# Stage six of an eight-stage transformer kernel: token rows gathered by an inverse list instead of sent to slots, and the shared expert squared and kept by ScalarE

## The chip, the cores and the metric

The kernel runs on one core of one Trainium2 chip as a single program. The metric is device microseconds (us) of one execution; lower is better. The kernel before was timed three times: 1947.86, 1949.66 and 1950.64 us, median 1949.66.

## The reference, cut to what matters

The whole program is four layers of attention and feed-forward blocks over a residual `x` of 4 batches x 512 tokens x 256 features in f32. The change is in the feed-forward block of the third layer, the program's sixth stage: a mixture of experts with a shared expert, on layer-normed tokens.

```python
logits = x @ w_router.T                       # 2048 tokens, 8 experts
probs = softmax(logits)
expert_weight, expert_idx = top_k(probs, 2)
expert_weight = expert_weight / sum(expert_weight, axis=-1)
# tokens sorted by expert; each expert e, on its own tokens:
inter = square(relu(x_e @ w1[e].T))           # 256 -> 256
outb  = inter @ w2[e].T                       # 256 -> 256
moe_out = zeros.at[token].add(outb * weight)  # two contributions a token
sh = square(relu(h @ ws1.T))                  # 256 -> 512, every token
shared_out = sh @ ws2.T                       # 512 -> 256
return shared_out + moe_out                   # added to the residual
```

The eighth stage is another mixture of experts (gated, 704 hidden features) with the same routing of 2 out of 8.

## The kernel before, in words

Each engine runs its own instruction list in order, and semaphores tie the lists together. The stages follow one another with a barrier of all engines between them. `core.x`, the residual, stays in SBUF; PSUM is one tensor `ps` of 8 banks of 512 f32 columns.

Stage six is `relu_experts_stage` (L2348). The 2 x 2048 choices are laid out in blocks of N = 256 slots, each block of one expert; K = 23 blocks always run, so that any distribution fits.

- **Router** (L1941, unchanged): layer norm of 16 token tiles into `kept_rows`, transposes into `xT`, logits, softmax, the two best. VectorE then computes in `Slots.vector_places` (L2265 to L2312) each choice's slot, each block's expert (`expert_no`, semaphore `experts_known`) and a copy of each token row for each of its two choices (`out_rows`: 256 features, the destination number, the weight; 32 instructions at L2312).
- **Sending**: GpSimd (`pool_send`, L2166) scatters these with 32 indirect DMAs of 128 rows into `xs_rows` in device memory. Unused slots must hold valid spare numbers, so stage five fills all of `xs_rows` from the constant `blank_rows` (L1635) beforehand. SyncE waits for all 32 and then loads each block of 256 rows (`xs`, L2109).
- **The shared expert** is cut into 8 units (half of the hidden features x a batch). `shared_first(u)` (L2414) is 4 f32 matmuls of 512 columns into banks 0 and 1; ScalarE takes relu (L2481), VectorE squares (L2526); `shared_second(u)` (L2425) is 8 f32 matmuls into banks 4 to 7; VectorE adds each tile to the residual (L2536). Six units (`FRONT`) run before the block loop and two behind it. TensorE's order is first(1), second(0), first(2), second(1), and so on.
- **The block loop**, software pipelined, per block k on TensorE: `up(k+1)` (L2445), the transposes of block k+2 (L2209), `down(k)` (L2456). ScalarE: relu (`gate`, L2490) of k+1, then the weighted result of k (L2499). VectorE: the square of k+1 (`product`, L2548), then two tiny copies of numbers and weights (L2319, L2321) and the tokens of k+2 to SBUF (L2551). GpSimd: a cast of the numbers (L2174) and two indirect DMAs that write the results of k to `y_rows` (L2179), so 46 in all. SyncE: per block one load of w1, one of w2, one of xs. The loops are hardware loops with register indices.
- **Collecting**: after the last write SyncE loads `y_rows` back in 8 loads of 512 KB (L2153); VectorE adds them to the residual (L2343), in order behind the additions of the shared units.

Stage eight uses another class, `Places` (L2563), which sends no rows. SyncE writes the normed rows once, in order, to `xn_rows` (L2620). VectorE marks for each choice its tile and its lane as f16 zeros and ones (`tile_is`, `lane_is`); TensorE's `tensor_inverse` (L2660) turns them into inverse lists with 32 matmuls for the numbers (L2667) and 32 for the weights (L2673), the latter from three f16 parts that GpSimd makes (`pool_weights`, L2632 to L2643). Results are `x_no` (which token row each slot reads), `y_no` (where its result goes) and `weight_of`. GpSimd then gathers each block's rows with two indirect DMAs (`gather`, L2858), four blocks ahead, and writes the block's results with two more (`give_back`, L2865), all in one unrolled list.

Of the kernel before, what the change touches and what calls it, by code (L numbers as in the profile page):

```python
# [20 lines left out]
P = 128  # L21
B = 4
# [1528 lines left out]
def autocorrelation_stage(core):  # L1551
# [19 lines left out]
    with Stage(core, "l2x") as st:  # L1571
# [30 lines left out]
        out_full, rows_added, cleared = st.sem("out_full"), st.sem("rows_added"), st.sem("rows_cleared")  # L1602
# [6 lines left out]
        def _(sp):  # L1609
# [25 lines left out]
            sp.dma_start(dram["xs_rows"], dram["blank_rows"]).then_inc(cleared, 16)  # L1635
# [8 lines left out]
            sp.wait_ge(cleared, 16)  # L1644
# [396 lines left out]
class Slots:  # L2041

    E = 8
    T = B * TT
    N = 2 * P
    K = (2 * T * P + E * (N - 1)) // N
    W = D + 2
    LOOPED = (K - 2) // 2

    def __init__(self, st, router, scaled):  # L2060

        T, E, K, W, N = self.T, self.E, self.K, self.W, self.N
        U32 = mybir.dt.uint32
        self.nc, self.core, self.router, self.scaled, self.dram = st.nc, st.core, router, scaled, st.core.dram
        self.earlier, self.ones = st.sb("earlier", [P, P]), st.sb("ones", [P, P])
        self.numbers = st.sb("numbers", [P, T, 2])
        self.starts = st.sb("starts", [P, E])
        self.block_no = st.sb("block_no", [P, K])
        self.y_in = st.sb("y_in", [P, 2, T, D])
        self.slot, self.is_second = (st.sb(n, [P, T, E]) for n in ("slot", "is_second"))  # L2070
        self.sums = st.sb("sums", [P, 2, T, E])
        self.filled = st.sb("filled", [P, E, E])
        self.blocks, self.ends, self.counts = st.sb("blocks", [P, E]), st.sb("ends", [P, 2, E]), st.sb("counts", [P, E])
        self.ended = st.sb("ended", [P, K, E])
        self.expert, self.expert_no = st.sb("expert", [P, K]), st.sb("expert_no", [P, K], I32)
        self.slots, self.slot_no = st.sb("slots", [P, T, 2]), st.sb("slot_no", [P, T, 2], U32)
        self.slot_sum = st.sb("slot_sum", [P, T])
        self.weight = st.sb("weight", [P, T, 2])
        self.out_rows = st.sb("out_rows", [P, T, 2, W])
        self.xs = st.sb("xs", [P, 2, 2, W])  # L2080
        if not scaled:
            self.xT = st.sb("xT_block", [P, 2, DC, N])
        self.y = st.sb("y", [P, 2, 2, D])
        self.numbers_of, self.weight_of = st.sb("numbers_of", [P, K, 2]), st.sb("weight_of", [P, K, 2])
        self.row_no = st.sb("row_no", [P, 2, 2], U32)
        self.const_in, self.ones_ready = st.sem("const_in"), st.sem("ones_ready")
        self.placed, self.ranks_full, self.experts_known = st.sem("placed"), st.sem("ranks_full"), st.sem("experts_known")
        self.rows_ready, self.scattered = st.sem("rows_ready"), st.sem("scattered")
        self.xs_in = [st.sem(f"xs_in{i}") for i in range(2)]
        self.turned, self.xT_ready = st.sem("turned"), st.sem("xT_ready")  # L2090
        self.y_ready, self.row_no_ready = st.sem("y_ready"), st.sem("row_no_ready")
        self.y_out = [st.sem(f"y_out{i}") for i in range(2)]
        self.y_back = [st.sem(f"y_back{b}") for b in range(B)]
        self.added = st.sem("added")

    def sync_constants(self, sp):
        dram = self.dram
        for dst, name in ((self.earlier, "earlier"), (self.numbers, "choice_numbers")):  # L2100
            sp.dma_start(dst[:], dram[name]).then_inc(self.const_in, 16)
        sp.dma_start(self.starts[:], dram["block_starts"].to_broadcast([P, self.E])).then_inc(self.const_in, 16)
        sp.dma_start(self.block_no[:], dram["block_numbers"].to_broadcast([P, self.K])).then_inc(self.const_in, 16)

    def sync_expert(self, sp, k):
        return sp.value_load(self.expert_no[0:1, bass.ds(k, 1)], min_val=0, max_val=self.E - 1)

    def sync_tokens(self, sp, r, i):
        sp.dma_start(self.xs[:, i, :, :],  # L2109
                     self.dram["xs_rows"][bass.ds((r * 2 + i) * self.N, self.N), :].rearrange("(j p) d -> p j d", p=P)  # L2110
                     ).then_inc(self.xs_in[i], 16)

    def sync_blocks(self, sp, first, second):

        K = self.K

        def second_of(r, i):
            second(self.sync_expert(sp, r * 2 + i), r, i)

        def step(r, i, left=3):
            first(self.sync_expert(sp, r * 2 + i), r, i)
            if left > 1:
                sp.wait_ge(self.xT_ready, r * 2 + i)
                self.sync_tokens(sp, r + i, 1 - i)
            second_of(r - 1 + i, 1 - i)

        sp.wait_ge(self.experts_known, 1)
        first(self.sync_expert(sp, 0), 0, 0, wait=False)
        second_of(0, 0)
        first(self.sync_expert(sp, 1), 0, 1, wait=False)
        sp.wait_ge(self.scattered, 2 * self.T * 16)
        for i in range(2):
            self.sync_tokens(sp, 0, i)
        sp.wait_ge(self.xT_ready, 1)
        self.sync_tokens(sp, 1, 0)
        with sp.Fori(1, (K - 1) // 2) as r:  # L2140
            for i in range(2):
                step(r, i)
        for k in range((K - 1) // 2 * 2, K):
            step(k // 2, k % 2, left=K - k)
        second_of((K - 1) // 2, (K - 1) % 2)

    def sync_collect(self, sp):
        for i in range(2):
            sp.wait_ge(self.y_out[i], 32 * ((self.K + 1 - i) // 2))
        for b in range(B):  # L2150
            for c in range(2):
                at = (c * B + b) * S
                sp.dma_start(self.y_in[:, c, b * TT:(b + 1) * TT, :],  # L2153
                             self.dram["y_rows"][at:at + S, :].rearrange("(j p) d -> p j d", p=P)).then_inc(self.y_back[b], 16)

    def pool_ones(self, pool):
        self.nc.gpsimd.memset(self.ones[:], 1.0).then_inc(self.ones_ready, 1)
        pool.wait_ge(self.ones_ready, 1)  # L2160

    def pool_send(self, pool):
        for t in range(self.T):
            pool.wait_ge(self.rows_ready, t + 1)
            for c in range(2):
                self.nc.gpsimd.indirect_dma_start(  # L2166
                    self.dram["xs_rows"], bass.IndirectOffsetOnAxis(ap=self.slot_no[:, t, c:c + 1], axis=0),
                    self.out_rows[:, t, c, :], None).then_inc(self.scattered, 16)

    def pool_return(self, pool, r, i):  # L2170
        k = r * 2 + i

        pool.wait_ge(self.y_ready, k + 1 + 2)
        self.nc.gpsimd.tensor_copy(self.row_no[:, i, :], self.numbers_of[:, bass.ds(k, 1), :].rearrange("p o j -> p (o j)")  # L2174
                                   ).then_inc(self.row_no_ready, 1)
        pool.wait_ge(self.row_no_ready, k + 1)
        pool.nop(nofuse=True)
        for c in range(2):
            self.nc.gpsimd.indirect_dma_start(  # L2179
                self.dram["y_rows"], bass.IndirectOffsetOnAxis(ap=self.row_no[:, i, c:c + 1], axis=0),  # L2180
                self.y[:, i, c, :], None).then_inc(self.y_out[i], 16)

    def pool_return_all(self, pool):
        with pool.Fori(0, self.K // 2) as r:
            for i in range(2):
                self.pool_return(pool, r, i)
        for k in range(self.K // 2 * 2, self.K):
            self.pool_return(pool, k // 2, k % 2)

    def tensor_ranks(self, pe):

        nc, ps, TE = self.nc, self.core.ps, self.T * self.E
        pe.wait_ge(self.const_in, 64)
        pe.wait_ge(self.ones_ready, 1)
        pe.wait_ge(self.placed, 1)
        nc.tensor.matmul(ps[:, 3, 0:TE], self.earlier[:], self.router.chosen[:].rearrange("p t e -> p (t e)"),
                         start=True, stop=False)
        nc.tensor.matmul(ps[:, 3, 0:TE], self.ones[:], self.sums[:, 1].rearrange("p t e -> p (t e)"), start=False, stop=True)  # L2200
        nc.tensor.matmul(ps[:, 4, 0:self.E], self.ones[:], self.sums[:, 0, self.T - 1, :], start=True, stop=True
                         ).then_inc(self.ranks_full, 1)
# [143 lines left out]


def relu_experts_stage(core):  # L2348

# [1359 lines left out]
```

## Time and profile before

| what | value |
|---|---|
| median of the three timed runs | 1949.66 us |
| the profiled execution, its own time | 1950.97 us |
| its span | 1949.2 us |
| TensorE busy / VectorE / ScalarE / GpSimd | 1621.0 / 1039.4 / 851.6 / 527.2 us |
| mean granted TensorE clock | 0.898 |
| stage six, first to last instruction | 688.9 to 910.3 us |

Times in the profile are microseconds from the span's start. PE is TensorE's matmuls, PEld its weight loads, DVE VectorE, ACT ScalarE, POOL GpSimd, SP SyncE; L2445 is line 2445 of the kernel. The chain of waits that ended last is followed back only as far as 1577 us, into stage eight, so stage six has to be read from its own timeline. In a windows row the columns are: stretch, its length, busy microseconds (and instructions) of PE, PEld, DVE, ACT and POOL, then granted TensorE clock (1.00 is 2.4 GHz, 0.50 is 1.2 GHz), DMA share and GB/s.

### The profile page before, as it was taken

The numbers are of one execution on the slowest core, as the hardware profiler recorded it, in microseconds if no ns is written. First come the engines' busy times: TensorE is split into PE (matmuls) and PEld (weight loads), VectorE is DVE, ScalarE is ACT, GpSimd is POOL, SyncE is SP. The second block draws the span as 40 slices with busy tenths as digits, with TensorE's granted clock in tenths as the row PEclk, the third lists the DMA queues.
The fourth block names the chain that finished last, engine by engine and source line by source line (L and its number), as shares of the span: only waits on it lengthen the run. The fifth ranks groups of instructions, "written<-read, shape, count | busy, mean of one in ns | idle before, by whom it ended". The sixth has DMA issues, their size and how long they took to land. (4 is left out here: it accounts for less than half of the span.)

```text
span 1949.2 us, 30637 instructions
## 1 busy us (share of the span) xinstructions
PE 1621.0 (83%) x10659; PEld 1079.1 (55%) x10662; DVE 1039.4 (53%) x2717; ACT 851.6 (44%) x1771; POOL 527.2 (27%) x564
## 2 busy tenths in 40 slices
PE   6999549782569968894899999999999973999994
PEld 2233238561246555673456656746756673888883
DVE  6543464557764155336586377378456536444443
ACT  2767203033512111231577277367557611555551
POOL 2000100001251007342337108206504505233321
PEclk8999866895889969997899999999999975999997
DMA  3000200201070103686213104203302213677785
GB/s 124 1 1 1 68 11 1 86 1 45 1 251 23 38 24 104 197 250 207 80 40 131 48 1 139 80 1 105 125 1 70 81 47 103 219 239 239 230 232 169
DMA packets 90977, 185.91 MB, mean 95 GB/s; under 512 B 10560, under 2 KB 56512, under 8 KB 90504
## 3 DMA queue, kind: packets, MB, share of 16 engines
q1 hardware_dynamic: 73320, 125.85, 19.9%
q0 software_dynamic: 17536, 58.51, 8.9%
q8 instruction: 68, 1.11, 0.2%
q14 instruction: 53, 0.43, 0.1%
HBM read 146.01 MB, written 44.40 MB: 98 GB/s over the span
## 5 line engine op out<-in xcount | busy, mean ns | idle before, releaser
L3452 ACT ACTIVATE l3x_prob<-l3x_biased,l3x_neg_max 128x512 f32<-128x512 f32 x256 | 183.8, 721 | 39.3 <-DVE l3x_neg_max L3548 35.7
L3548 DVE CUSTOM_DVE_ANT_0 l3x_biased<-ps,l3x_mask 128x512 f32<-128x512 f32 x256 | 173.4, 681 | 13.6 <-PE ps L3326 6.8
L2907 PE MATMUL ps<-l3f_x_hi,l3f_w 128*128 128x256 f16 x1012 | 171.5, 274 | 3.8 <-DVE l3f_x_lo L3034 2.4
L402 ACT ACTIVATE l0x_prob<-ps 128x1024 f32<-128x1024 f32 x128 | 122.6, 1027 | 80.1 <-PE ps L347 80.0
L3336 PE MATMUL ps<-ident,l3x_prob 128*128 128x128 f32 x1024 | 142.0, 282 | 1.1 <-ACT l3x_prob L3452 1.0
L2907 PE MATMUL ps<-l3f_x_lo,l3f_w 128*128 128x256 f16 x506 | 138.8, 274 | 0.0
L3461 ACT ACTIVATE l3x_probT<-ps 128x512 f32<-128x512 f32 x192 | 112.1, 586 | 42.2 <-PE ps L3336 42.2
L3352 PE MATMUL ps<-l3x_probT,l3x_v 128*64 128x256 f32 x1024 | 124.6, 385 | 5.0 <-ACT l3x_probT L3461 5.0
L3336 PEld LDWEIGHTS ps<-ident,l3x_prob 128*128 128x128 f32 x1024 | 111.3, 142 | 27.8 <-issue 21.2
L3023 DVE TENSOR_TENSOR l3f_h<-l3f_silu,ps 128x256 f32<-128x256 f32 x115 | 48.4, 421 | 141.0 <-ACT l3f_silu L2972 140.9
L2907 PEld LDWEIGHTS ps<-l3f_x_hi,l3f_w 128*128 128x128 f16 x1012 | 99.6, 98 | 18.8 <-issue 4.4
L2921 PE MATMUL ps<-l3f_w,l3f_h_hi 128*128 128x256 f16 x552 | 96.2, 274 | 0.0
L2865 POOL DMA_INDIRECT y_rows<-l3f_y,l3f_y_no x46 | 45.4, 988 | 181.9 <-ACT l3f_y L2981 174.9
L3352 PEld LDWEIGHTS ps<-l3x_probT,l3x_v 128*64 128x64 f32 x1024 | 67.8, 136 | 47.3 <-issue 11.8
L3559 DVE COPY l3x_probT<-ps 128x512 f32<-128x512 f32 x64 | 44.2, 690 | 88.7 <-PE ps L3336 87.8
L3323 PE MATMUL ps<-l3x_k_hi,l3x_q 128*128 128x512 f16 x256 | 78.0, 386 | 13.2 <-DVE l3x_neg_max L3548 13.1
L2972 ACT ACTIVATE l3f_silu<-ps 128x256 f32<-128x256 f32 x138 | 52.7, 382 | 82.2 <-PE ps L2907 80.6
L3249 PE MATMUL ps<-l3x_x_hi,l3x_w 128*128 128x512 f16 x256 | 82.6, 384 | 0.0
L3092 POOL TENSOR_TENSOR l3x_raw_parts<-l3x_raw,l3x_raw_parts 128x1088 f16<-128x1088 f32 x32 | 72.2, 2256 | 2.7
L367 PE MATMUL ps<-l0x_prob,l0x_v 128*32 128x512 f32 x512 | 68.0, 604 | 3.0 <-DVE l0x_oT L456 2.5
L3426 ACT ACTIVATE l3x_q<-ps 64x512 f16<-64x512 f32 x64 | 37.8, 591 | 61.0 <-PE ps L3249 60.6
L3220 POOL CAST l3x_o_hi<-l3x_o 128x256 f16<-128x256 f32 x64 | 28.1, 439 | 131.4 <-DVE l3x_o L3530 131.4
(611 smaller groups left out, 3669.8 us busy)
## 6 DMA issues: line engine op xcount, KB each, us to landing
l3f_w<-l3f_parts SPq DMA_DIRECT2D x23, 1408.0 KB, 6.8
l3f_w<-l3f_parts SPq DMA_DIRECT2D x23, 768.0 KB, 6.3
l3x_raw<-in_l3f_weights POOLq DMA_DIRECT2D x32, 544.0 KB, 4.0
l3f_parts<-l3x_raw_parts POOLq DMA_DIRECT2D x32, 544.0 KB, 3.2
l2f_w<-in_l2f_w SPq DMA_DIRECT2D x46, 256.0 KB, 3.1
xs_rows<-in_blank_rows SPq DMA_DIRECT2D x1, 5934.0 KB, 25.3
l2f_xs<-xs_rows SPq DMA_DIRECT2D x23, 258.0 KB, 3.3
l2f_y_in<-y_rows SPq DMA_DIRECT2D x8, 512.0 KB, 7.0
```

Source lines behind the costliest of these rows:

```text
L367: last = nc.tensor.matmul(ps[r:r + 32, AV_BANK, :], values[:, b % 2, j, 4 * g + head, :, :], probs[:, head, :], start=(j == 0 and at == 0) ...
L402: nc.scalar.activation(prob[:, n % KEPT, 2 * h:2 * h + 2, :], ps[:, bank:bank + 2, :], ACT.Sigmoid, scale=0.25).then_inc(prob_ready, 1)
L2907: last = nc.tensor.matmul(ps[:, f % RING, g * N:(g + 1) * N], w13[:, i, part, c * 2 * F + at:c * 2 * F + at + P], x[:, i, c, :], start=(n ...
L2921: last = nc.tensor.matmul(ps[:, 4 + i, j * D:(j + 1) * D], hT[0:m, i, f, j * P:(j + 1) * P], w2[0:m, i, part, f * D:(f + 1) * D], start=(n ...
L3092: G.tensor_tensor(lo, raw, hi, ALU.subtract).then_inc(self.lo_made, 1)
L3249: last = nc.tensor.matmul(out, a, b, start=(begin and n == 0), stop=(end and n == len(passes) - 1))
L3323: nc.tensor.matmul(ps[:, (u + i) % 3, :], q2[:, 2 * hp + i, tile], k_hi[:], start=True, stop=False)
L3336: last = nc.tensor.transpose(ps[:, turned_bank(unit), s * P:(s + 1) * P], prob[:, unit % 4, s * P:(s + 1) * P], core.ident[:])
L3352: last = nc.tensor.matmul(ps[rows, av_bank(group), 0:HALF].rearrange("p (j q) -> p j q", j=2), v[:, s, :], probT[:, group % 2, :, i, s * P ...
L3452: nc.scalar.activation(prob[:, unit % 4, :], biased[:, unit % 4, :], ACT.Exp, scale=-1.0, bias=neg_max[:, u // 4, u % 4:u % 4 + 1], accum_ ...
L3461: nc.scalar.activation(prob_slot(made), ps[:, turned_bank(made), :], ACT.Copy).then_inc(copied[0], 1)
L3548: V.tensor_tensor_reduce(out=biased[:, unit % 4, :], in0=ps[:, u % 3, :], in1=mask[:, u % 8 // 2, :], scale=-1.0, scalar=3.0e38, op0=ALU.a ...
```

## The change: what it does

Class `Slots` goes, and with it `xs_rows`, its blank fill in stage five, the 32 sends, the 32 row copies, the 23 loads of `xs` and the per-block copies and casts of numbers. Stage six now uses `Places`, whose `tensor_inverse` is split into two calls, with the bank of the numbers as a parameter. The order of the shared units is now by batch (both halves of a batch one after the other, summed in PSUM); ScalarE squares as well, and copies the sum of a batch out of PSUM (`keep`) once per batch; VectorE adds that copy once per batch. All loops but SyncE's are written out. The last units and the collection stay where they were.

```diff
@@ stage five
-            sp.dma_start(dram["xs_rows"], dram["blank_rows"]).then_inc(cleared, 16)
-            sp.wait_ge(cleared, 16)
@@ class Places
-    def tensor_inverse(self, pe):
+    def tensor_numbers(self, pe):
...
+    def tensor_weights(self, pe):
@@ relu_experts_stage, GpSimd
+            def gather(k):
+                if k >= AHEAD:                       # AHEAD = 4
+                    pool.wait_ge(turned, k - AHEAD + 1)
+                for j in range(2):
+                    nc.gpsimd.indirect_dma_start(
+                        gathered[:, k % AHEAD, j, :], None, dram["xn_rows"],
+                        bass.IndirectOffsetOnAxis(ap=places.x_no[:, 2 * k + j:2 * k + j + 1], axis=0)).then_inc(rows_in[k % AHEAD], 16)
+            def give_back(k):
+                pool.wait_ge(y_ready, k + 1)
+                for j in range(2):
+                    nc.gpsimd.indirect_dma_start(
+                        dram["y_rows"], bass.IndirectOffsetOnAxis(ap=places.y_no[:, 2 * k + j:2 * k + j + 1], axis=0),
+                        y[:, k % 2, j, :], None).then_inc(y_out[k % 2], 16)
+            places.pool_ones(pool)
+            router.pool(pool)
+            places.pool_weights(pool)
+            pool.wait_ge(places.rows_out, 16 * B)
+            pool.wait_ge(places.numbers_known, 1)
+            for k in range(AHEAD):
+                gather(k)
+            for k in range(K):
+                if k + AHEAD < K:
+                    gather(k + AHEAD)
+                give_back(k)
@@ TensorE
+            for u in range(FRONT):
+                if u + 1 < FRONT:
+                    shared_first(u + 1)
+                shared_second(u)
+                if u == 3:
+                    places.tensor_numbers(pe)
+                if u == 4:
+                    places.tensor_weights(pe)
+            pe.wait_ge(shared_kept, FRONT // 2)
...
+            turn(0)
+            up(0)
+            turn(1)
+            for k in range(K):
+                if k + 1 < K:
+                    up(k + 1)
+                if k + 2 < K:
+                    turn(k + 2)
+                down(k)
+            pe.wait_ge(relu_ready, K)
+            shared_first(FRONT)
+            pe.wait_ge(y_ready, K)
+            for u in range(FRONT, UNITS):
+                if u + 1 < UNITS:
+                    shared_first(u + 1)
+                shared_second(u)
@@ ScalarE
+            def hidden(u):
+                for f in range(FT):
+                    n = u * FT + f
+                    act.wait_ge(shared_up, n + 1)
+                    A.activation(relu[:, u % 2, f, :], ps[:, n % 2, :], ACT.Relu).then_inc(shared_relu, 1)
+                ...
+                for f in range(FT):
+                    A.activation(hT[:, u % 2, f, :], relu[:, u % 2, f, :], ACT.Square).then_inc(shared_hidden, 1)
+            def keep(b):
+                act.wait_ge(shared_down, 2 * b + 2)
+                bank = 4 + b % 2 * 2
+                A.activation(shared_rows[:, b, :, :], ps[:, bank:bank + 2, :]..., ACT.Copy).then_inc(shared_kept, 1)
+            def result(k):
+                act.wait_ge(down_full, k + 1)
+                if k >= 2:
+                    act.wait_ge(y_out[k % 2], k // 2 * 32)
+                ...
@@ VectorE, behind places.vector_places
+            for b in range(FRONT // 2):
+                add_shared(b)                        # waits for shared_kept, b + 1
+            tokens(0)
+            product(0)
+            tokens(1)
+            for k in range(K - 1):
+                product(k + 1)
+                if k + 2 < K:
+                    tokens(k + 2)
+            for b in range(FRONT // 2, B):
+                add_shared(b)
+            dve.wait_ge(shared_added, B)
+            for b in range(B):
+                dve.wait_ge(y_back[b], 32)
+                ...                                  # two additions of y_in, as before
@@ SyncE: per block w1 once up(k-2) is done, then w2 once down(k-2) is done
```

## Rows read from the trace of the kernel before

**Rows 1.** The windows view of stage six: microseconds busy per engine, clock, DMA.

```profile
748.40:779.50 31.10, 31.10 (x113) 21.04 (x111) 13.60 (x28) 4.78 (x8) 23.49 (x23) 1.00 0.29 103
...
791.00:885.10 94.10, 92.71 (x445) 75.09 (x446) 31.35 (x85) 31.58 (x66) 44.43 (x64) 1.00 0.77 233
885.10:910.30 25.20, 13.78 (x49) 8.78 (x47) 15.85 (x20) 3.23 (x6) 4.39 (x5) 0.82 0.57 187
```

**Rows 2.** The timeline (start, us, engine, line, what) of the shared expert's front.

```profile
730.89 5.16 PE L2414 MATMUL ps<-l2f_xT,l2f_ws 128*128 128x512 f32 x8 [2.97 <-DVE l2f_expert_no L2292]
...
742.17 6.34 PE L2425 MATMUL ps<-l2f_ws,l2f_hT_shared 128*128 128x256 f32 x16 [6.12 <-DVE l2f_hT_shared L2526]
...
755.23 3.60 PE L2414 MATMUL ps<-l2f_xT,l2f_ws 128*128 128x512 f32 x8
...
762.12 3.60 PE L2414 MATMUL ps<-l2f_xT,l2f_ws 128*128 128x512 f32 x8
```

**Rows 3.** The timeline where the block loop begins: first transposes, first return.

```profile
783.36 1.09 PE L2209 MATMUL ps<-ident,l2f_xs 128*128 128x128 f32 x4 [3.85 <-DMA l2f_xs<-xs_rows]
...
797.29 0.96 POOL L2179 DMA_INDIRECT y_rows<-l2f_y,l2f_row_no  x1 [0.79 <-POOL l2f_row_no L2174]
```

**Rows 4.** The timeline of one block of stage six in the steady loop.

```profile
803.71 2.00 PE L2445 MATMUL ps<-l2f_xT_block,l2f_w 128*128 128x256 f32 x8
...
805.74 0.60 ACT L2490 ACTIVATE l2f_relu<-ps 128x512 f32<-128x512 f32 x1 [1.00 <-PE ps L2445]
...
806.37 0.69 DVE L2548 TENSOR_TENSOR l2f_hT<-l2f_relu 128x512 f32<-128x512 f32 x1 [2.72 <-ACT l2f_relu L2490]
...
807.12 0.68 DVE L2551 COPY l2f_xT_block<-ps 128x512 f32<-128x512 f32 x1
...
807.86 1.99 PE L2445 MATMUL ps<-l2f_xT_block,l2f_w 128*128 128x256 f32 x8
...
808.09 0.84 ACT L2499 ACTIVATE l2f_y<-ps,l2f_weight_of 128x256 f32<-128x256 f32 x2 [1.75 <-PE ps L2456]
```

**Rows 5.** Stage eight's timeline: first and last of four consecutive indirect DMAs.

```profile
1684.79 1.00 POOL L2865 DMA_INDIRECT y_rows<-l3f_y,l3f_y_no  x1 [6.92 <-ACT l3f_y L2981]
...
1688.67 0.96 POOL L2858 DMA_INDIRECT l3f_gathered<-xn_rows,l3f_x_no  x1 [0.30 <-issue]
```

**Rows 6.** The eighth stage's gather line (L2858): time from issue to landing.

```profile
DMA to landing us min/median/max: 2.7/3.6/4.6
```

**Rows 7.** The timeline where an indirect DMA starts inside a two-input VectorE product.

```profile
759.50 0.69 DVE L2526 TENSOR_TENSOR l2f_hT_shared<-l2f_relu_shared 128x512 f32<-128x512 f32 x1 [1.02 <-ACT l2f_relu_shared L2481]
759.61 1.41 POOL L2166 DMA_INDIRECT xs_rows<-l2f_out_rows,l2f_slot_no  x1 [0.30 <-issue]
```

**Rows 8.** Stage eight's timeline: experts' numbers, then the list-making matmuls.

```profile
1618.55 0.18 DVE L2713 TENSOR_SCALAR l3f_expert_no<-l3f_expert 128x23 int32<-128x23 f32 x1
...
1637.24 1.41 PE L2667 MATMUL ps<-l3f_marked_values,l3f_lane_is 128*128 128x92 f16 x16 [3.18 <-DVE l3f_lane_is L2748]
...
1639.76 3.86 PE L2673 MATMUL ps<-l3f_marked_values,l3f_lane_is 128*128 128x138 f16 x32 [1.11 <-POOL l3f_marked_values L2643]
```

**Rows 9.** The windows view of a stretch of the list-making matmuls.

```profile
1639.70:1643.70 4.00, 3.86 (x32) 3.58 (x32) 0.00 (x0) 0.00 (x0) 2.74 (x4) 0.50 0.17 49
```

**Rows 10.** The page: a two-bank ScalarE read, and the expert weight loads.

```profile
L402 ACT ACTIVATE l0x_prob<-ps 128x1024 f32<-128x1024 f32 x128 | 122.6, 1027 | 80.1 <-PE ps L347 80.0
...
l2f_w<-in_l2f_w SPq DMA_DIRECT2D x46, 256.0 KB, 3.1
```

**Rows 11.** The windows view of stage five while the blank fill runs.

```profile
575.00:580.00 5.00, 5.00 (x18) 3.11 (x17) 2.89 (x10) 0.87 (x3) 4.23 (x4) 1.00 0.95 342
```

**Rows 12.** The timeline of stage six's end.

```profile
884.94 7.03 PE L2414 MATMUL ps<-l2f_xT,l2f_ws 128*128 128x512 f32 x16
...
892.70 7.39 SPq L2153 DMA_DIRECT2D l2f_y_in<-y_rows  x8
...
907.77 2.48 DVE L2343 TENSOR_TENSOR x_sb<-x_sb,l2f_y_in 128x1024 f32<-128x1024 f32 x2 [0.44 <-DMA l2f_y_in<-y_rows]
```

More of the change, by code:

```diff
@@ L1601, in autocorrelation_stage @@
         agg_full, agg_by_act, agg_by_vector = st.sem("agg_full"), st.sem("agg_by_act"), st.sem("agg_by_vector")
-        out_full, rows_added, cleared = st.sem("out_full"), st.sem("rows_added"), st.sem("rows_cleared")
+        out_full, rows_added = st.sem("out_full"), st.sem("rows_added")
         block = st.block()
@@ L2575, with __init__ @@
     PARTS = 5
-    def __init__(self, st, router):
+    def __init__(self, st, router, numbers_bank=5):
         T, E, K = self.T, self.E, self.K
+        self.numbers_bank = numbers_bank
         U32 = mybir.dt.uint32
@@ L2666, in tensor_inverse @@
                 pe.wait_ge(self.lanes_marked, n // T + 1)
-            last = nc.tensor.matmul(ps[:, 5, 0:4 * K], self.lane_is[:, n, :],
+            last = nc.tensor.matmul(ps[:, self.numbers_bank, 0:4 * K], self.lane_is[:, n, :],
                                     self.marked[:, n, 0:2, :].rearrange("p v k -> p (v k)"),
@@ L2670, in tensor_inverse @@
         last.then_inc(self.numbers_full, 1)
+    def tensor_weights(self, pe):
+        nc, ps, K, T = self.nc, self.core.ps, self.K, self.T
         pe.wait_ge(self.weights_marked, 3)
@@ L2752, in vector_places @@
         dve.wait_ge(self.numbers_full, 1)
-        token, second = ps[:, 5, 0:2 * K], ps[:, 5, 2 * K:4 * K]
+        bank = self.numbers_bank
+        token, second = ps[:, bank, 0:2 * K], ps[:, bank, 2 * K:4 * K]
         V.tensor_scalar(self.x_no[:], token, -1.0, 0.0, ALU.add, ALU.max)
@@ L2886, in _ @@
             places.tensor_ranks(pe)
-            places.tensor_inverse(pe)
+            places.tensor_numbers(pe)
+            places.tensor_weights(pe)
             def turn(r, i):
```

611 lines of the change are left out of this document (184 added, 427 removed).

## The prediction

> **What bounds the kernel now.** The page's chain of waits is followed back only into stage eight, so I read stage six by the windows view first and then by its timeline. The windows [rows 1] show three stretches with different limits. While the shared expert's front runs (748.4 to 779.5) TensorE is busy all the time at full clock. In the block loop (791.0 to 885.1) it is busy 92.7 of 94.1 us, while GpSimd is busy 44.4: TensorE and the VectorE link into it set the pace. Behind it (885.1 to 910.3) TensorE works 13.8 of 25.2 us, and the write-back and its re-load end last. Two stalls lie ahead of the loop: 6.12 us before second(0), which waited for VectorE's square behind the 32 row copies [rows 2], and 3.85 us before the first transposes, which waited for the sends and the load of xs [rows 3].
>
> One block's circle reads as follows [rows 4]: up starts 803.71, relu 805.74 to 806.34, square 806.37 to 807.06, two tiny copies, tokens 807.12 to 807.80, next up 807.86. One round is 4.15 us.
>
> **The front, until the first return.** experts_known doesn't move: the instructions ahead of it are the same but for constants. From there on:
> - first(1): 730.89 + 5.16 (half of it at the low clock) = 736.05 [rows 2].
> - second(0) follows at once, since ScalarE has squared unit 0 long before. One unit (first and second) takes 762.12 - 755.23 = 6.89 us, 3.60 of it first, so second takes 3.29 [rows 2]: 739.3. Before, it began at 742.17 and took 6.34, cold; here TensorE has not rested, and the level holds (the windows give 1.00 for unbroken work [rows 1]).
> - Three units: 20.7, so 760.0.
> - The 32 matmuls for the numbers: 2 x 1.41 = 2.8 us in stage eight, those for the weights 3.86 [rows 8]. That was at clock 0.50 [rows 9], the 1.2 GHz level; at 2.4 GHz no row shows them. Between half of it and all of it, I take half (the stretch around them runs at 1.00): 1.4 and 1.9. Their inputs: in stage eight the second half waited for VectorE until 1637.24, 18.5 us after the experts' numbers (1618.73), and the weights for GpSimd until 1639.76, 21.0 us after [rows 8]; here 29 and 37 us pass, so neither waits: 761.4.
> - first(5) and second(4) 6.9, weights 1.9, second(5) 3.3: 773.5.
> - keep(2): a two-bank ScalarE read, nearest row 1.03 us [rows 10] and 0.2 for the hand-over: 774.8, and TensorE may start turn(0). VectorE adds batch 2 (one of the two halves of the 2.48 us in [rows 12], 1.24), copies tokens (0.68, [rows 4]): up(0) at 776.9.
> - One round to up(1), one to the end of down(0): 785.2. Result 0.84 [rows 4] and 0.2: 786.2. GpSimd's first return starts at 786.4 instead of 797.29 [rows 3]: 10.9 us gained. Uncertain by +3.3 us (lists at the low clock) and some 0.5 the other way.
>
> Squares on ScalarE appear in no row; nearest is the relu of 0.60 [rows 4]. Two of them behind a relu are 1.8 us, and first(u+1) covers 3.6. Even at double price they are hidden. Without that cover each of the 8 units would pay up to 2 us.
>
> **The block loop.** Here the change adds what costs most. GpSimd had two indirect DMAs and a cast per block; now it has four indirect DMAs. In stage eight four in a row start at 1684.79 and 1688.67, the last 0.96 long with 0.30 to the next: 1689.93 - 1684.79 = 5.14 us [rows 5]. In stage six one takes 0.96, so four would be 5.04 [rows 3]. Both are above TensorE's 4.15, so GpSimd becomes the bound. I take 5.14, the row with the same mix. The wait for y_ready(k) has gather(k+4) behind it, which TensorE's turn(k+4) needs only four blocks later, and y_out(k-2) lands well within two rounds, so GpSimd isn't starved in mid-loop. The two tiny copies that VectorE loses (0.14 a round) and the xs load that SyncE loses bring nothing, as they lie beside GpSimd. SyncE now asks for w1 only behind w2, a wait of down(k-2) instead of up(k-1): landing 3.1 us [rows 10] within a round of 5.14 leaves 2 us for its register loads.
>
> From 786.4 GpSimd does 18 returns and 18 gathers (blocks 5 to 22): 18 x 5.14 = 92.5, so 878.9. The last gather, issued 1.26 earlier, lands 3.6 later [rows 6]: 881.2. TensorE's part of a round is up 2.0 and turn with down 2.15 (together 4.15, [rows 4]); a down alone is half of a second, 1.7 [rows 2]. turn(22) and down(20) 2.15, up(22) 2.0, down(21) 1.7, down(22) 1.7: 888.8. y_ready(21) comes at 887.1 + 1.0 = 888.1; four more DMAs behind it, 5.1: 893.3. Before, the last ended 891.2, 1.5 ahead of SyncE's re-load at 892.70 [rows 12]. So the 10.9 us are used up and 2.1 more.
>
> **The end.** The re-load starts at 894.8; its last part was awaited until 15.1 us after its start (907.77 - 892.70 [rows 12]), so 909.9. But shared units 6 and 7 come behind down(22) on TensorE: before it began them at 884.94 [rows 12], now at 888.8. 13.8 us for both [rows 1]: 902.6. Then keep(3) 1.2 (903.8) and VectorE's addition 1.24 (905.0), and only behind it the eight additions, 4 x 2.48 = 9.9 [rows 12]: 914.9 instead of 910.25. Those additions were spaced by landings before; now VectorE sets the end.
>
> Stage five loses the blank fill, but its TensorE was busy 5.00 of 5.00 us in the middle of it [rows 11]: nothing to gain. Bounds 0 to -1.
>
> **Sum.** Against the profiled execution (1950.97, span 1949.2): -10.9 front, +13.0 loop, +2.6 end = +4.7, 1955.7. It lay 1.3 above the median of the runs, so 1949.66 + 4.7 = 1954.4. A change within 0.2% (3.9 us) is about what a measurement can't tell from none.
>
> **Rivals.**
> A. *VectorE holds GpSimd up as well, slower still.* An indirect DMA that starts 0.11 us into a VectorE product with both inputs in SBUF took 1.41 instead of 0.96 [rows 7]. In the loop the square is such a product, 0.69 us a round. Starts come every 1.28, so with free phase about every second round is hit for 0.3: 18 x 0.14 = +2.5; if the phase locks on it, 18 x 0.45 = +8.1. For: the square follows the landing of gathers, so the phase is fixed by GpSimd itself. Against: the return in [rows 3] and the gather in [rows 5] have 0.96, and the sum's 5.14 may hold some of it already. Time 1957 to 1962.5.
> The Trainium skill (GPSIMD Engine Reference, section Key points) says the same: contention of the shared SBUF interfaces arises with VectorE instructions that have two SBUF inputs; by that rule alone the time would be the upper one, 1962.5, if every round is hit. [Rows 7] agree in one instance.
> B. *The other side: GpSimd doesn't bound.* It would have to overlap issue with the next DMA, or hold the lead of its four early gathers. Then the round is 4.0 (4.15 less what the tiny copies took): y_ready(22) = 786.2 + 22 x 4.0 = 874.2, down(22) 873.2, units 887.0, end 899.3, thus -10.9 and 1939. It decides from a round below 4.88 (18 x 0.26 = 4.7 cancels my sum). Against: in no row do two indirect DMAs start less than 1.25 apart.
> C. *The front gives less:* lists at the low clock and cold first blocks, 3.3 to 4 us: 1958.
> D. *Equal:* DMAs at 1.25 (round 5.0, -2.5) and up to 1 us less at the end, if keep and additions come cheaper: 1951.
>
> **Chances.** Forecast 0.47 (own range 1952 to 1958), A 0.20, B 0.10, C 0.10, D 0.13. Faster than 1945.8: B and a little of other cases, 0.12. Within 0.2%: most of D and the lower part of the forecast, up to 1953.6, 0.27. Slower: 0.61. The range to hold 8 in 10: 1947 to 1964.
>
> **What would show it.** Right: in the loop GpSimd nearly always busy, with 1.25 to 1.3 between starts and rounds of 5.0 to 5.3; TensorE's clock and busy share down, with waits for gathered rows or for ScalarE's result; no 6.12 us stall ahead of second(0); first return near 786; VectorE's eight additions in one piece of 10 us behind keep(3). Wrong: rounds below 4.8 us; list matmuls that wait for VectorE or GpSimd; ScalarE's squares on TensorE's waits; a w1 load awaited; stage five shorter by more than 1 us.

## The result and the profile after

The changed kernel takes 1962.75 us (median; 1962.5 to 1963.14) against 1949.66 before: a ratio of 1.0069, 95% interval 1.0046 to 1.0092. Run again with more rounds it came to 1.0055 (1.0042 to 1.0069). So it is slower by 11 to 13 us, where +4.7 was predicted. Direction and cause of the forecast hold; its size is less than half of what happened. The 1962.75 lies in the range given for 8 in 10 (1947 to 1964) and outside the forecast's own (1952 to 1958).

A stage's length is read from its first layer-norm instruction to that of the next stage. The view by tile gives them, for the kernel before (first pair) and the changed one (second pair); the number ahead of "to" is the first start in us.

```profile
L117 DVE BATCH_NORM_STATS2 l2f_bn<-x_sb x16: 407/409/428, 689.0 to 699.3; 128x6 f32<-128x256 f32 x16
L117 DVE BATCH_NORM_STATS2 l3x_bn<-x_sb x16: 395/408/427, 911.5 to 1309.7; 128x6 f32<-128x256 f32 x16
```

```profile
L117 DVE BATCH_NORM_STATS2 l2f_bn<-x_sb x16: 408/410/428, 687.7 to 698.1; 128x6 f32<-128x256 f32 x16
L117 DVE BATCH_NORM_STATS2 l3x_bn<-x_sb x16: 395/409/428, 922.8 to 1321.4; 128x6 f32<-128x256 f32 x16
```

Stage six went from 222.5 to 235.1 us, 12.6 more; in its second run 232.1, with the blank fill put back (below) 233.1. The mean of the three is 233.4: +10.9. What follows the stage has the same length, 1037.7 and 1037.6 us. What precedes it varies by 4.6 us from run to run whatever the kernel (685.2 to 689.8 over all runs here), so times below are compared from the stage's own start.

The windows view of the changed kernel answers to [rows 1]: start and end, length, busy us (instructions) of PE, PEld, DVE, ACT, POOL, then clock, DMA share, GB/s. The windows are the shared front, the block loop and the end.

```profile
729.80:775.20 45.40, 44.21 (x200) 29.97 (x200) 21.82 (x34) 14.23 (x23) 25.40 (x16) 0.94 0.17 47
790.00:880.00 90.00, 74.61 (x352) 59.81 (x353) 22.28 (x35) 25.36 (x53) 68.54 (x69) 0.98 0.69 200
881.50:921.50 40.00, 25.32 (x95) 18.24 (x93) 13.08 (x12) 10.04 (x19) 9.78 (x11) 0.85 0.55 167
```

TensorE, busy 92.7 of 94.1 us in the old loop, is now busy 74.6 of 90. GpSimd has 69 instructions there; 68.54 busy and 0.30 between each two (69 x 0.30 = 20.7) make 89.2 of the 90 us, so it is the engine that hardly rests.

The timeline of the front, to be read against [rows 2, 3]: second(0) follows first(1) without the stall of 6.12, the matmuls for the numbers start at 760.23, and the first return at 786.53. But first(1) takes 6.40 instead of 5.16.

```profile
729.88 6.40 PE L2368 MATMUL ps<-l2f_xT,l2f_ws 128*128 128x512 f32 x8 [2.98 <-DVE l2f_expert_no L2194]
736.12 3.62 PE L2379 MATMUL ps<-l2f_ws,l2f_hT_shared 128*128 128x256 f32 x16
...
760.23 1.48 PE L2144 MATMUL ps<-l2f_marked_values,l2f_lane_is 128*128 128x92 f16 x32
763.39 1.19 POOL L2332 DMA_INDIRECT l2f_gathered<-xn_rows,l2f_x_no  x1 [12.57 <-DVE l2f_y_no L2241]
774.13 1.02 ACT L2463 ACTIVATE l2f_shared_rows<-ps 128x1024 f32<-128x1024 f32 x1 [7.25 <-PE ps L2379]
775.21 0.66 PE L2401 MATMUL ps<-ident,l2f_gathered 128*128 128x128 f32 x4 [1.11 <-ACT l2f_shared_rows L2463]
...
786.53 1.01 POOL L2339 DMA_INDIRECT y_rows<-l2f_y,l2f_y_no  x1 [8.04 <-ACT l2f_y L2484]
```

The windows view of first(1), before and after, shows why: after the same 3 us of rest the mean granted clock is 0.56 instead of 0.71, so more of it ran at the 1.2 GHz level.

```profile
730.89:736.05 5.16, 5.15 (x8) 2.06 (x8) 4.88 (x23) 0.60 (x1) 1.20 (x1) 0.71 0.43 118
```

```profile
729.88:736.10 6.22, 6.22 (x8) 2.66 (x9) 5.74 (x19) 0.60 (x1) 2.89 (x5) 0.56 0.51 148
```

The timeline inside the loop: two returns and two gathers a block, and the next block's first return 5.2 us later. One return of 1.49 us starts 0.07 into VectorE's product with two SBUF inputs, as in [rows 7].

```profile
814.63 0.69 DVE L2525 TENSOR_TENSOR l2f_hT<-l2f_relu 128x512 f32<-128x512 f32 x1 [3.07 <-ACT l2f_relu L2476]
814.70 1.49 POOL L2339 DMA_INDIRECT y_rows<-l2f_y,l2f_y_no  x1 [0.30 <-issue]
...
829.75 1.00 POOL L2339 DMA_INDIRECT y_rows<-l2f_y,l2f_y_no  x1 [0.30 <-issue]
831.05 0.99 POOL L2339 DMA_INDIRECT y_rows<-l2f_y,l2f_y_no  x1 [0.30 <-issue]
832.35 0.99 POOL L2332 DMA_INDIRECT l2f_gathered<-xn_rows,l2f_x_no  x1 [0.30 <-issue]
833.64 1.03 POOL L2332 DMA_INDIRECT l2f_gathered<-xn_rows,l2f_x_no  x1 [0.30 <-issue]
834.98 1.00 POOL L2339 DMA_INDIRECT y_rows<-l2f_y,l2f_y_no  x1 [0.31 <-issue]
```

TensorE's waits from 775 to 905 (us in total, times, longest). The loads of w1 come first. The prediction had dismissed them, and had named an awaited w1 load among the signs that it was wrong:

```profile
PE ps L2412 <- DMA l2f_w<-in_l2f_w: 12.5, 12, 3.0
PE ps L2401 <- DMA l2f_gathered<-xn_rows,l2f_x_no: 5.5, 6, 1.7
```

The timeline of the end, against [rows 12]: w1 of block 21 is asked for at 878.97, 1.22 us behind a load of w2; up(21) waits for it until 884.25 and then runs partly at the low level, the last return is over at 899.5 instead of 891.2, and the eight additions run in one piece behind keep(3) and the shared addition.

```profile
877.75 0.38 SPq L2305 DMA_DIRECT2D l2f_w<-in_l2f_w  x1
...
878.97 0.38 SPq L2299 DMA_DIRECT2D l2f_w<-in_l2f_w  x1
...
881.81 1.00 POOL L2339 DMA_INDIRECT y_rows<-l2f_y,l2f_y_no  x1 [0.31 <-issue]
...
884.25 2.57 PE L2412 MATMUL ps<-l2f_xT_block,l2f_w 128*128 128x256 f32 x8 [2.27 <-DMA l2f_w<-in_l2f_w]
...
898.53 0.97 POOL L2339 DMA_INDIRECT y_rows<-l2f_y,l2f_y_no  x1 [0.30 <-issue]
...
901.01 0.38 SPq L2323 DMA_DIRECT2D l2f_kept_rows<-y_rows  x1
...
909.12 1.02 ACT L2463 ACTIVATE l2f_shared_rows<-ps 128x1024 f32<-128x1024 f32 x1 [5.27 <-PE ps L2379]
910.18 1.23 DVE L2513 TENSOR_TENSOR x_sb<-x_sb,l2f_shared_rows 128x1024 f32<-128x1024 f32 x1 [16.93 <-ACT l2f_shared_rows L2463]
911.44 1.22 DVE L2544 TENSOR_TENSOR x_sb<-x_sb,l2f_kept_rows 128x1024 f32<-128x1024 f32 x1
...
920.26 1.23 DVE L2544 TENSOR_TENSOR x_sb<-x_sb,l2f_y_second 128x1024 f32<-128x1024 f32 x1
```

### The profile page after: what moved, and what is told of

Read it like the earlier page. It is cut to its first block and busy times, and to the rows that moved or that the text cites. A ratio compares the mean times of both kernels' runs of the same rounds, so it can differ in the third digit from the quotient of the medians.

```text
span 1960.4 us, 30184 instructions
## 1 busy us (share of the span) xinstructions
PE 1625.3 (83%) x10723; PEld 1084.1 (55%) x10726; DVE 1026.8 (52%) x2612; ACT 865.3 (44%) x1791; POOL 554.1 (28%) x563
## 5 line engine op out<-in xcount | busy, mean ns | idle before, releaser
L137 POOL TENSOR_TENSOR l3x_rstd<-l3x_var,neg_half 128x4 f32<-128x4 f32 x4 | 4.1, 1036 | 214.9 <-DVE l3x_var L124 214.9
```

## The experiments

Each starts from the changed kernel. Ratios are to the kernel before, timed beside it on the same chip; "length" is that of stage six, from each run's own trace (before 222.5, changed 233.4 as the mean of three). A length is one execution, and the three of the changed stage lie 3.0 us apart, so small differences are read from the ratios.

| run | ratio, 95% interval | length |
|---|---|---|
| changed, again | 1.0055 [1.0042, 1.0069] | 232.1 |
| w1 asked first | 1.0059 [1.0045, 1.0073] | 231.9 |
| one-input product | 1.0055 [1.0039, 1.0070] | 233.2 |
| blank fill back | 1.0048 [1.0033, 1.0064] | 233.1 |
| VectorE squares | 1.0153 [1.0137, 1.0168] | 250.8 |
| 8 gather buffers | 1.0038 [1.0024, 1.0051] | 229.5 |
| half the gathers | 1.0009 [1.0000, 1.0018] | 222.9 |
| half the gathers, w1 first | 0.9940 [0.9925, 0.9956] | 210.9 |
| deep | 0.9984 [0.9975, 0.9993] | 218.2 |
| deep, 4 units ahead | 0.9949 [0.9936, 0.9963] | 211.3 |
| the same, w1 late | 0.9996 [0.9987, 1.0005] | 221.7 |
| the same, w1 first, 7 y buffers | 0.9916 [0.9903, 0.9930] | 205.8 |

**The changed kernel again**

> The changed kernel itself once more, to have its ratio to the kernel before from more rounds: the runs that undo one part of it (the fill 1.0048, the w1 order 1.0059) lie inside the interval of its first measurement, 1.0046 to 1.0092. Expected 1.0055 to 1.0070, stretches of 1.1 to 1.5 us on five to eight of the indirect DMAs of the loop, and 18 rounds in 94.5 to 96 us. If it comes out at 1.0048 or less, the fill and the w1 order at the loop's end are worth nothing that can be measured.

1.0055; 18 rounds of GpSimd in 94.3 us, from 784.23 to 878.52, just under the 94.5 to 96 expected. The first measurement's profile was on the long side, by 3 us of stage length. The ratio of this run lies within the intervals of the next three and theirs within its own, so none of the three moved the time measurably.

**w1 asked for before w2**

```diff
+            first(1, 0)
             with sp.Fori(1, K // 2) as r:
                 for i in range(2):
-                    first(r, i)
+                    first(r + i, 1 - i)
                     second(r, i)
             for k in range(K // 2 * 2, K):
-                first(k // 2, k % 2)
                 second(k // 2, k % 2)
```

> SyncE asks for w1 of block k+1 before w2 of block k, as the kernel before did; all else is the changed kernel. Theory G (GpSimd's four indirect DMAs, 5.17 us a round, set the loop, and the w1 order costs only at its end): TensorE's waits for w1 go from 12.5 us to under 2 us, the gaps turn into waits for rows or for GpSimd, the returns still come every 5.17 us, and only the end of the loop gains, 2 to 5 us: 1958 to 1961. Rival W (the late w1 sets the round): the returns come every 4.2 to 4.6 us and the time falls by 10 us or more, to 1952 or less. Rival V (VectorE's product holds GpSimd up): no change but the end's.

TensorE's waits for w1 are gone. The same idle time stands at the next thing it needs:

```profile
PE ps L2401 <- DMA l2f_gathered<-xn_rows,l2f_x_no: 16.3, 10, 3.0
```

12.5 + 5.5 = 18.0 us of waiting became 16.3. Most returns still come every 5.17 (18 rounds in 94.1, so 5.23 in the mean), and the time doesn't move: 12.5 us at the top of a list of waits were worth nothing, because TensorE isn't the bound. From the 19th round's start to the end of the last return it is 15.4 us (879.56 to 895.01) instead of 16.1 to 17.7: the end gains 1 to 2 us at most, less than the 2 to 5 that I expected.

**One SBUF input in VectorE's product**

```diff
-  V.tensor_tensor(hT_b[:, k % 2, :, :], relu_b[:, k % 2, :, :], relu_b[:, k % 2, :, :], ALU.mult)
+  V.scalar_tensor_tensor(out=hT_b[:, k % 2, :, :], in0=ps[:, k % 2, :].rearrange("p (f n) -> p f n", f=FT),
+                         scalar=0.0, in1=relu_b[:, k % 2, :, :], op0=ALU.max, op1=ALU.mult)
```

> VectorE's product of a block takes one input from PSUM (max(up, 0) times the kept relu) instead of two from SBUF; same numbers result. Theory G: the seven stretched indirect DMAs (1.17 to 1.49 us) become 0.97 to 1.0, about 2 us less in the loop: 1960 to 1962. Rival V (the two-input product is what sets the round of 5.29): the round falls to 4.9 or less and the time by 6 us or more.

The returns by line (min/median/max ns), changed kernel first, then this one:

```profile
L2339 POOL DMA_INDIRECT y_rows<-l2f_y,l2f_y_no x46: 971/994/1491, 786.5 to 898.5; - x46
```

```profile
L2339 POOL DMA_INDIRECT y_rows<-l2f_y,l2f_y_no x46: 967/987/1009, 784.2 to 894.2; - x46
```

Not one return is stretched any more, so in this loop the stretches come from the two-input product. Whether it meets a DMA depends on the phase: in the run with half the gathers and w1 first, below, the same two-input product stretches none of the loop's DMAs. The time stays at 1.0055, where I expected some 2 us less. The stretches had summed to 1.6 us in the 18 rounds, and this run has instead one wait of GpSimd for a result, which was 0.94 in the changed kernel and absent when that was run again:

```profile
811.73 1.00 POOL L2339 DMA_INDIRECT y_rows<-l2f_y,l2f_y_no  x1 [2.04 <-ACT l2f_y L2484]
```

**The blank fill back in stage five**

```diff
+            sp.dma_start(dram["xs_rows"], dram["blank_rows"]).then_inc(cleared, 16)
 ...
+            sp.wait_ge(cleared, 16)
```

> The changed kernel with the blank fill back in stage five (the DRAM-to-DRAM copy and its wait at the stage's end). Theory: the fill was hidden, the time is that of the changed kernel within 1 us. Rival (the fill's removal gave or took time in stage five): 1.5 us or more of difference either way.

1.0048, inside the intervals of the changed kernel; stage five is 136.2 us with the fill (138.2 in the kernel before, which has it too) and 135.6 to 138.3 without it in twelve runs. The fill was hidden, within what can be told.

**The shared squares back on VectorE**

```diff
-    A.activation(hT[:, u % 2, f, :], relu[:, u % 2, f, :], ACT.Square).then_inc(shared_hidden, 1)
+    V.tensor_tensor(hT[:, u % 2, f, :], relu[:, u % 2, f, :], relu[:, u % 2, f, :], ALU.mult).then_inc(shared_hidden, 1)
 ...
+        between(0)
         dve.wait_ge(self.numbers_full, 1)
```

`between(0)` is the squares of units 0 to 4; those of unit 5 follow the numbers.

> The changed kernel with the shared expert's squares back on VectorE, behind its making of the list and ahead of what reads the list (units 0 to 4 ahead, 5 behind the numbers); nothing else is changed. Theory: VectorE is busy with the list until 748.3, so TensorE's second(0) moves from 736.1 to about 749.8, and all of the front and the loop moves with it: first return at 799 to 801 instead of 786.5, 12 to 14 us more than the changed kernel. Rival (the front gained from the sends that are gone, not from ScalarE's squares): under 4 us more.

TensorE's second(0), behind VectorE's making of the list:

```profile
750.63 5.53 PE L2381 MATMUL ps<-l2f_ws,l2f_hT_shared 128*128 128x256 f32 x16 [15.80 <-DVE l2f_hT_shared L2512]
```

It waits 15.80 us, and, rested, takes 5.53 instead of 3.62 at the lower level. From the stage's start the first return comes after 116.5 us instead of 98.8: 17.7 later, and the stage is 17.4 longer. The expected 12 to 14 left out the clock, and that the four squares took VectorE 4.95 us, not 2.8: the longest, begun beside GpSimd's marking, took 3.14, where the median is 0.68. Moving the squares to ScalarE is thus what lets the list be made at no price. That holds against squares behind the whole list; squares placed between its steps were not tried.

**Half of the gathers, without and with w1 first**

```diff
-                for j in range(2):
+                for j in range(1):
                     nc.gpsimd.indirect_dma_start(
                         gathered[:, k % AHEAD, j, :], ...
 ...
-                pe.wait_ge(rows_in[k % AHEAD], (k // AHEAD + 1) * 32)
+                pe.wait_ge(rows_in[k % AHEAD], (k // AHEAD + 1) * 16)
 ...
-                                                   gathered[:, k % AHEAD, j, c * P:(c + 1) * P], core.ident[:])
+                                                   gathered[:, k % AHEAD, 0, c * P:(c + 1) * P], core.ident[:])
```

Both kernels leave out half of the token rows: TensorE transposes the first gather's rows twice. So they serve to measure only.

> Leaves out the second gather of every block (TensorE turns the first one's rows twice), so that GpSimd issues three indirect DMAs a round instead of four, 3.86 us. Theory G: TensorE with its late w1 sets the round at 4.3 to 4.7 us, and the time falls by 10 to 17 us, to 1946 to 1953. Rival W: under 3 us. Rival V: the stretches stay, and the fall is the same as under G.

> Leaves out the second gather of every block, as the half-gathers run did, and asks for w1 before w2. Theory now (two limits lie close together: GpSimd's 5.17 us round, and behind it TensorE with its late w1 at 4.6 us, as the half-gathers run's 18 rounds in 83.0 us show): with both gone the round is TensorE's own, 4.15 to 4.25 us, 18 rounds in about 76 us, and the time is 5 to 8 us under that of the half-gathers run: 0.2 to 0.4% below the kernel before. Rival (something else, such as y's two buffers or the landing of the returns, holds the round at 4.6): no change against the half-gathers run.

Ratios 1.0009 and 0.9940. The first return and that of the 19th block, without (first fence) and with w1 first (second):

```profile
786.53 1.01 POOL L2339 DMA_INDIRECT y_rows<-l2f_y,l2f_y_no  x1 [9.29 <-ACT l2f_y L2484]
...
869.55 0.99 POOL L2339 DMA_INDIRECT y_rows<-l2f_y,l2f_y_no  x1 [1.09 <-ACT l2f_y L2484]
```

```profile
784.79 1.01 POOL L2339 DMA_INDIRECT y_rows<-l2f_y,l2f_y_no  x1 [9.29 <-ACT l2f_y L2484]
...
857.29 0.98 POOL L2339 DMA_INDIRECT y_rows<-l2f_y,l2f_y_no  x1 [0.47 <-ACT l2f_y L2484]
```

18 rounds: 94.9 us with all gathers (mean of the three), 83.0 with half, 72.5 with half and w1 early. So there are three limits one behind another: GpSimd at 5.27 a block, SyncE's order with w1 at 4.61 (TensorE waited for it 16 times), and TensorE itself at 4.03. The last gain, 12 us, is more than the 5 to 8 I expected. (The 74.5 that a later expectation gives is a misreading of this 72.5.)

**Eight gather buffers**

```diff
-    AHEAD = 4
+    AHEAD = 8
```

> Eight gather buffers instead of four, all else the changed kernel: eight DMAs move from the loop into GpSimd's idle time before the first return (773.6 to 786.5). Theory G: 14 or 15 rounds at 5.17 us, then only returns at TensorE's pace (about 4.2 us); y has two buffers, so TensorE can't run ahead and the gain is 3 to 5 us: 1958 to 1960. Rival W: nothing, 1962 to 1963. Rival V: as G, a little more.

1.0038, and 3.9 us off the stage, within what was expected, though some 0.7 of it is the front (first return after 97.8 us instead of 98.5), which this edit doesn't touch. GpSimd works without a pause until 865, and from there y's two buffers and w1 hold the returns at 3.9 to 5.2 us a block.

**Deep: 8 gather buffers, 4 for y, w1 first**

```diff
-    AHEAD = 4
+    AHEAD = 8
+    YB = 4
 ...
-        y = st.sb("y", [P, 2, 2, D])
+        y = st.sb("y", [P, YB, 2, D])
 ...
-                if k >= 2:
-                    act.wait_ge(y_out[k % 2], k // 2 * 32)
+                if k >= YB:
+                    act.wait_ge(y_out[k % YB], k // YB * 32)
```

> All work kept: eight gather buffers, four buffers for y, and w1 asked before w2. Theory: GpSimd works on without a pause from the first gather (763.4) and has 92 indirect DMAs of 1.285 us, to about 883 to 886; TensorE runs at 4.15 to 4.3 us a block from 777 and ends the blocks at 877 to 880, the two shared units then end by 893, and the last eight additions start at about 895 instead of 911.4: 14 to 18 us less than the changed kernel, 0 to 0.3% below the kernel before. Rival (a depth of buffers doesn't help, since GpSimd's total sets the end in any case): the gain is no more than that of the eight gather buffers alone, about 6 us.

0.9984, and 15.2 us off the stage, as expected. GpSimd issued all 92 indirect DMAs without a pause, from 763.19 to 884.8, and the additions begin at 895.76. That is 1.322 us for each DMA: without slack on GpSimd the stretches do count, by up to 3.8 us against the 1.281 of the next kernel, which has the one-input product. What that product alone is worth here was not run.

```profile
763.19 1.19 POOL L2333 DMA_INDIRECT l2f_gathered<-xn_rows,l2f_x_no  x1 [11.53 <-DVE l2f_y_no L2241]
...
883.85 0.97 POOL L2340 DMA_INDIRECT y_rows<-l2f_y,l2f_y_no  x1 [0.30 <-issue]
```

**Four shared units ahead of the blocks, four behind**

```diff
-    FRONT = 6
+    FRONT = 4
 ...
                     shared_first(u + 1)
-                shared_second(u)
-                if u == 3:
+                if u == 2:
                     places.tensor_numbers(pe)
-                if u == 4:
-                    places.tensor_weights(pe)
+                shared_second(u)
+            places.tensor_weights(pe)
 ...
-            for b in range(FRONT // 2, B):
-                add_shared(b)
-            dve.wait_ge(shared_added, B)
             for b in range(B):
+                if b >= FRONT // 2:
+                    add_shared(b)
+                dve.wait_ge(shared_added, b + 1)
                 dve.wait_ge(y_back[b], 32)
```

This comes on top of the deep kernel (8 gather buffers, 4 for y, w1 first), with VectorE now adding batch by batch, and it also has the one-input product; what each of these is worth by itself was not run. One more run puts w1 back behind w2, and another gives y seven buffers (`YB = 7`).

> All work kept: the deep kernel with VectorE's one-input product, only four shared units ahead of the blocks (the numbers made before second(2), the weights after second(3), the other four units behind the blocks), and VectorE adding batch by batch. Theory (GpSimd's 92 indirect DMAs of 1.28 us are the stage's longest chain once the buffers are deep, so what counts is when the first gather starts): gathers start at 755 to 757 instead of 763.4, TensorE's first block at 762 to 764, GpSimd's last return at 874 to 878, TensorE's shared units end at about 892, the additions of batches 0 and 1 are hidden beside them and the stage ends at 898 to 902, about 20 us before the changed kernel's 921.5: 0.3 to 0.5% below the kernel before. Rival (TensorE's total, with 28 us of shared work now behind the blocks, is what ends the stage): no better than the deep kernel, 1.0 to 0.998.

> The deep kernel with four shared units ahead (0.9949 of the kernel before), with one thing put back: w1 asked after w2, as the changed kernel does. Theory: in the changed kernel the late w1 is hidden by GpSimd's 5.17 us round (asking early gave 1.0059 against 1.0055, nothing), but where GpSimd no longer holds TensorE, a block costs it 4.6 us instead of 4.2 to 4.4, as the half-gathers pair showed (18 rounds in 83.0 against 74.5 us). Here TensorE's shared units end the stage, so 23 blocks at 0.2 to 0.4 us more are 5 to 9 us more than the four-ahead kernel: 0.997 to 1.0. Rival (the order is worth nothing): 0.995, within 2 us.

> The four-ahead kernel with seven buffers for y instead of four. In it ScalarE waited 3 to 5 us a block for a return to land before it could write y, and TensorE 6.2 us in 6 waits behind it, and its blocks took 4.38 us each. Theory: TensorE's blocks come down to 4.1 to 4.2 us, its shared units and with them the stage end 4 to 6 us earlier, GpSimd's last return stays where it is: 0.992 to 0.993 of the kernel before. Rival (TensorE is held by something else): 0.995, no change.

0.9949, at the better end of what was expected: the gathers start at 750.60 (expected 755 to 757), and GpSimd is done with all 92 DMAs at 868.44, 1.281 us each. The waits view shows what then holds ScalarE, four buffers for y:

```profile
ACT l2f_y L2484 <- DMA y_rows<-l2f_y,l2f_y_no: 25.9, 7, 5.1
```

With w1 late the same kernel falls back to 0.9996, 9 us (10.4 in stage length), at the upper end of what was expected; TensorE's waits there:

```profile
PE ps L2412 <- DMA l2f_w<-in_l2f_w: 15.0, 17, 2.0
```

With seven buffers for y and w1 early it is 0.9916, a little better than the 0.992 to 0.993 expected (1932.61 us against 1948.66): 16 us faster than the kernel before, and by the two ratios (1.0055 - 0.9916 = 1.39%) some 27 us faster than the changed one. Its windows view (front, loop, end) shows TensorE busy 86.5 of 89 us in the loop beside a GpSimd that doesn't pause either:

```profile
727.60:757.00 29.40, 26.43 (x119) 18.05 (x120) 21.23 (x41) 7.71 (x13) 20.20 (x11) 0.88 0.16 43
768.00:857.00 89.00, 86.45 (x429) 71.67 (x428) 28.43 (x44) 30.67 (x64) 67.97 (x70) 0.99 0.78 225
857.00:895.00 38.00, 31.82 (x116) 21.61 (x114) 12.94 (x11) 13.25 (x23) 11.12 (x12) 0.96 0.50 161
```

## Why the prediction was right in direction and too small

**GpSimd becomes the bound: right.** The half-gathers run shows it: a quarter of the loop's DMAs gone, 10.5 us gone. A round without stretches is 5.17 us (the one shown above, 829.75 to 834.98, is longer and holds a stretch of 0.04), against the 5.14 taken from [rows 5].

**The front: right but for its clock.** Predicted from the stage's start: 786.4 - 689.0 = 97.4 us to the first return. Measured 98.4 to 98.8, mean 98.5. The step that was off is "first(1): 730.89 + 5.16": 6.40 here, at a clock of 0.56 instead of 0.71; 6.0 and 6.05 in the two other runs of the same stage. That the list and weights matmuls wait for nothing (1.48 and 2.09 us, predicted 1.4 and 1.9), that the squares on ScalarE are hidden, and that the sends' removal needs no price are right. Term: +1.1.

**Eighteen rounds: the mid-size term was too small.** Predicted 92.5, measured 94.3 to 95.3, mean 94.9. In the first profile of the changed kernel: 18 x 5.17 = 93.0, stretches by the two-input product 1.6, one wait for a result 0.6. The prediction knew the stretches, as rival A, and priced them at 2.5 at free phase, but left them out of the likeliest sum. Its own [rows 7] held the evidence, so they belonged in it. Term: +2.4.

**The loop's end: the step that failed.** "The last gather ... lands 3.6 later" took a median for the one landing on which the chain hangs. With w1 early and the chain otherwise as predicted, the transposes of block 22 started 4.9 us after that gather's start (4.7 in the changed kernel's second run), and the end took 15.4 instead of 14.4. "Landing 3.1 us within a round of 5.14 leaves 2 us for its register loads" was wrong as well. The prediction knew that w1 of block k+1 is asked for behind w2 of block k, and so behind down(k-2), but it priced neither the 1.22 us between the two asks (877.75 to 878.97) nor a landing above the median: w1 took 3.7 us in the median and 5.3 before up(21). TensorE waited for it 12 times. In mid-loop that is covered by GpSimd's round, so it cost nothing there (1.0059 against 1.0055); at the end, where the cover ends, up(21) waited 2.27 us and then ran slow for 2.57. Together 16.1 to 17.7, mean 16.7. Term: +2.3.

Of it 1.0 is the landing (w1 early: 15.4). The second run and the one with the fill have w1 late and a clock of 1.00 over this stretch, and take 16.1 and 16.3: 0.7 to 0.9 for w1. The first run, at 0.71, takes 17.7. The one-input run waited 1.89 us for w1 at the same up(21), kept 1.00 and took 16.4, so up to 1.3 of the first run is the clock. Each of these is one execution. The windows view of the stretch from up(21) on, first run and run with the fill:

```profile
884.20:890.00 5.80, 5.75 (x21) 4.82 (x22) 1.29 (x2) 0.60 (x1) 1.95 (x2) 0.71 0.63 189
```

```profile
881.10:886.90 5.80, 5.15 (x24) 4.09 (x25) 1.29 (x2) 1.48 (x4) 2.83 (x4) 1.00 0.67 194
```

**The end: right.** Eight additions in one piece behind keep(3), 23.3 us from the last return to the next stage; predicted 22.9. Term: +0.4.

1.1 + 2.4 + 2.3 + 0.4 = 6.2; measured 10.9 in stage length less the 4.7 predicted is 6.2 too. The misses are four, all of one sign: each term was the undisturbed one.

**The rivals.** A came nearest (1957 to 1962.5, against 1962.75 measured) by a mechanism that carries only 1.6 us of it: taking the stretches away left the time where it was. That its range, and the wide one for 8 in 10, reached the result is therefore in good part luck. The rule of the Trainium skill (GPSIMD Engine Reference, section Key points), that VectorE instructions with two SBUF inputs contend with GpSimd, is borne out by this case's runs: a longest return of 1.491 us with them, 1.009 without. B, that GpSimd doesn't bound, fell with the half-gathers run. C, the low clock in the front, was part of the truth (1.1 us), though at first(1) and not at the lists and first blocks where it was looked for. D, that the times come out equal, fell. Stage five: nothing, as predicted.

**What stays open.** Why stage five takes 136 us in most runs and 138 in some, with or without the fill, and why the clock rose later in first(1) in most runs than in the profile of the kernel before. The traces show that the two go together: stage five takes 137.8 to 138.3 in four of them (the kernel before, 8 gather buffers, deep, 7 y buffers), and in these first(1) takes 5.16 to 5.36; in the ten others stage five takes 135.6 to 136.5 and first(1) 6.00 to 6.59. So the miss of the front, about 1 us, goes with the execution that was profiled, and nothing here shows that the change causes it. It also flatters the lengths of those four by about as much.

## What to carry to other kernels

When an edit moves the bound to another engine, ask for the depth of every buffer between the two before giving the edit up: here four indirect DMAs a block cost 11 us with buffers of 4 and 2. With 8 and 4, and w1 asked early, the same edit gains 3 (0.9984); with two shared units moved behind the blocks, additions by batch and a one-input product as well, and 8 and 7 buffers, it gains 16. A wait at the top of an engine's list is worth nothing while another engine bounds (12.5 us of w1 waits: 0), and worth 9 us once that bound is gone. And a chain's last instance must not be priced at the median: here its landing (4.9 us against 3.6) and its wait for w1 were both longer, and no other engine's work covered them.

## What the hardware showed beside that

In these traces no two of GpSimd's indirect DMAs of 128 rows of 1 KB start less than 1.24 us apart, but with seven buffers for y they are issued for 118 us without a pause (92 of them at 1.281), most of that beside a TensorE that is busy 97% of the time, at a DMA share of 0.78 and 225 GB/s. The median time to landing stayed at 3.5 us for returns and 3.9 for gathers (3.5 and 3.6 in the changed kernel).
